# A fused two-layer Perceiver kernel: the first mixture's last eight experts in two token parts, and paired scores in the last attention

## The reference, cut to what matters

```
x = x + L0_xattn(norm(x), ctx64)     # 16 heads of 16, causal
x = x + L0_attn(norm(x))
x = x + L0_ffn(norm(x))              # mixture: 32 experts + 1 shared, top 4 of 32, silu(x W1) * (x W3) @ W2
x = x + L1_xattn(norm(x), ctx)       # 16 heads, ONE key/value head, 1601 keys per batch
x = x + L1_attn(norm(x))             # causal, 16 heads, layer norm with gamma and beta after it
x = x + L1_ffn(norm(x))              # mixture of 8 experts, gelu, top 1
```

## Time and profile before

| what | value |
|---|---|
| median of 3 runs | 552.41 us (551.35 to 553.02) |
| profiled execution, its own time | 552.53 us |
| its span, first to last instruction | 550.6 us |
| TensorE busy, share of the span | 94% |
| VectorE busy | 59% |
| ScalarE busy | 55% |
| GpSimd busy | 23% |
| mean granted TensorE clock | 0.996 |
| first mixture, steady part | 120 to 216 us of the span |
| cross attention, from its first scores | 241.35 to 400 us |
| last attention, scores to values | 415 to 442 us |

### The profile page before, as it was taken

How to read it: one execution, slowest core, us unless ns; L and a number is a source line. 1 busy time by engine, 2 the same in 40 slices (tenths; PEclk the granted TensorE clock), 3 DMA queues, 4 the chain that set the end, 5 groups by cost and what they waited for, 6 DMA issues and landing times.

```text
span 550.6 us, 15198 instructions
## 1 busy us (share of the span) xinstructions
PE 519.7 (94%) x6427; PEld 363.7 (66%) x6427; DVE 325.7 (59%) x672; ACT 300.3 (55%) x511; POOL 124.2 (23%) x217
## 2 busy tenths in 40 slices
PE   3999999889999999889999999999979999999997
PEld 2666567546665666435776767676556657999996
DVE  4455475276666665768999999998146685011011
ACT  0356566676656565358887777877714412432221
POOL 5203602644333333340000000000060043000004
PEclk9999999999999999999999999999999998999999
DMA  8914620805554453820000000000080001798823
GB/s 325 402 45 162 228 92 9 284 8 149 146 158 138 147 155 99 301 83 2 4 3 4 4 2 4 3 4 4 2 307 1 1 2 39 240 353 271 309 90 95
DMA packets 35074, 64.37 MB, mean 117 GB/s; under 512 B 3296, under 2 KB 24800, under 8 KB 34624
## 3 DMA queue, kind: packets, MB, share of 16 engines
q1 hardware_dynamic: 34480, 62.35, 34.3%
q0 software_dynamic: 384, 1.05, 0.6%
q10 hardware_dynamic: 144, 0.01, 0.0%
HBM read 59.40 MB, written 4.00 MB: 115 GB/s over the span
## 4 chain that ended last, share of the span: by engine, by line
PE 84%; DVE 8%; POOL 2%; DMA 2%; ACT 2%; issue 2%; SPq 0%; POOLq 0%; DVEq 0%; ACTq 0%
PE ps L1342 14%; PE ps L1612 10%; PE ps L1743 9%; PE ps L1711 8%; PE ps L1757 7%; PE ps L1626 7%; PE ps L1935 6%; PE ps L1443 4%; PE ps L1317 2%; PE ps L1456 2%; PE ps L1469 2%; PE ps L1423 2%; DVE region L1119 1%; DMA ctx64T<-in_ctx64T 1%; PE ps L1367 1%
## 5 line engine op out<-in xcount | busy, mean ns | idle before, releaser
L1119 DVE TENSOR_REDUCE region<-ps 128x1 f32<-128x512 f32 x192 | 124.1, 687 | 17.9 <-PE ps L1711 17.9
L807 ACT ACTIVATE region<-ps 128x1024 f32<-128x1024 f32 (+1 forms) x112 | 105.9, 963 | 19.7 <-PE ps L1743 19.2
L1711 PE MATMUL ps<-ctx_kT,region 96*32 96x512 bf16 x768 | 82.0, 383 | 2.5 <-DVE region L1119 1.8
L1743 PE MATMUL ps<-region,ctx_kT 98*32 98x512 bf16 x832 | 72.5, 381 | 0.6 <-ACT region L785 0.4
L1757 PE MATMUL ps<-region,ctx_v 128*32 128x128 f32 (+1 forms) x1664 | 70.2, 272 | 0.0
L1612 PE MATMUL ps<-region 128*128 128x512 f16 x264 | 62.9, 379 | 0.3 <-DMA region<-in_moe 0.3
L1757 PEld LDWEIGHTS ps<-region,ctx_v 128*32 128x32 f32 (+1 forms) x1664 | 56.7, 109 | 9.4 <-issue 0.3
L857 ACT ACTIVATE region<-ps,ctx_v 128x128 f32<-128x128 f32 x88 | 25.2, 369 | 60.8 <-PE ps L1342 60.8
L502 POOL TENSOR_TENSOR region<-region 128x512 f32<-128x512 f32 x33 | 38.2, 1157 | 64.7 <-ACT region L734 63.3
L1626 PE MATMUL ps<-region 128*128 128x256 bf16 x384 | 47.2, 273 | 0.9 <-DVE region L1066 0.9
L1626 PEld LDWEIGHTS ps<-region 128*128 128x128 bf16 x384 | 37.4, 98 | 12.3 <-DVE region L1066 1.5
(11 more groups left out here) (230 smaller groups left out, 839.9 us busy)
## 6 DMA issues: line engine op xcount, KB each, us to landing
region<-in_w SPq DMA_DIRECT2D x15, 1024.0 KB, 8.5
region<-in_ctxT SPq DMA_DIRECT2D x8, 1601.0 KB, 7.9
region<-gates SPq DMA_DIRECT2D x30, 256.0 KB, 3.4
ctx_kT<-in_w SPq DMA_DIRECT2D x7, 1024.0 KB, 7.3
region<-in_moe SPq DMA_DIRECT2D x33, 192.0 KB, 2.4
attn_weights<-in_wall SPq DMA_DIRECT2D x1, 2152.0 KB, 21.9
slots_x<-zeros SPq DMA_DIRECT2D x1, 1408.0 KB, 10.5
ctx_v<-in_b2row SPq DMA_DIRECT2D x1, 1024.0 KB, 4.6
```

The source lines that it names most:

```text
L807: act.activation(probs[u % NP_][:, 0:512 * n_keys], ps[:, pr:pr + n_keys, :].rearrange("p b n -> p (b n)"), ACT.Exp).then_inc(mq["exp"], 1)
L1119: ins = dve.tensor_reduce(mp[g % 2][:, j // 3, j % 3:j % 3 + 1], bank(4 + n % 2), AX.X, ALU.max)
L1711: ins = pe.matmul(ps[32 * i:32 * i + 32, at, :], QT[0:KQ, b, h + i // 2, 32 * (i % 2):32 * (i % 2) + 32], kT[0:KQ, b, 512 * c:512 * c + 51 ...
L1743: ins = pe.matmul(ps[32 * c:32 * c + 32, 2 * (u % 2) + i, :], kT[0:KQ2, b, k * P + 32 * c:k * P + 32 * c + 32], QT[0:KQ2, b, 8 * r:8 * r + ...
```

## The change

- The last `SPLIT` = 8 experts (25 to 32) are computed in two parts of 256 tokens: experts 0 to 24 whole, then 25 to 32 on tokens 0 to 255, then 25 to 32 on tokens 256 to 511. The program counts *items* i = 0 to 40 in the place of experts; `item(i)` gives the expert and the tokens. Their weights and gate rows get places of their own in `R1`, so that they stay for the second part; SP's loop over n is the same, with its wait on `m0["down"]` at n - 3.
- From item 28 on, PE runs `up(i)`, `down(i - 3)`.
- When item 32 (`A_LAST`) is done, tiles 0 and 1 are complete. DVE adds and measures tile 0 in item 35, tile 1 in item 36, scales them in items 37 and 38. PE turns tile 0 in item 39, ACT copies it there; `queries(0)` stands before `down(39)`, and the queries of tile 0 are split and turned before the last `down`.
- Tiles 2 and 3 are added and measured behind that; DVE scales them behind the first of the `maxima`.
- `chunks_by` has 15 chunks before unit 0, and 16 after it as before. Three of the six query turns (`EARLY_TURNS`) stand before unit 0, the other three in units 0 to 2. The 14 and 7 `keep_clock` matmuls around this place are gone.
- In the last attention, `pair_scores(g)` does the scores of two units at once, the units' 64-row halves in turns, and the orders of the three engines there are rearranged.

```diff
@@ sync
             for n in range(1, E0T):
+                if n == FULL:
+                    sp.wait_ge(kv["proj"], NB)
                 if n >= 4:
                     sp.wait_ge(m0["down"], n - 3)
-                    sp.dma_start(w0[n % 4], a["moe0"][n]).then_inc(w0_in[n % 4], 16)
+                    sp.dma_start(w0[place(n)], a["moe0"][n]).then_inc(w0_in[n % 4], 16)
                 if n > 2:
-                    sp.dma_start(gb[n % 4], scratch_g[n - 1:n, :].partition_broadcast(P)).then_inc(gb_in[n % 4], 16)
+                    sp.dma_start(gb[place(n)], scratch_g[n - 1:n, :].partition_broadcast(P)).then_inc(gb_in[n % 4], 16)
...
-            sp.wait_ge(m0["end"], 3)
+            sp.wait_ge(m0["end"], 2)
@@ vector, in the loop over the items, behind lo(i - 1)
+                if i == A_LAST + 3:
+                    dve.wait_ge(m0["end"], 1)
+                    dve.tensor_tensor(x[:, 0, :], sum0(0), x[:, 0, :], ALU.add).then_inc(m0["x"], 1)
+                    dve.wait_ge(m0["x"], 1)
+                    norms = [measure(x, 0, 1)]
+                if i == A_LAST + 4:
+                    dve.wait_ge(m0["down"], A_LAST + 1)
+                    dve.tensor_tensor(x[:, 1, :], sum0(1), x[:, 1, :], ALU.add).then_inc(m0["x"], 1)
+                    dve.wait_ge(m0["x"], 2)
+                    norms.append(measure(x, 1, 2))
+                if i == A_LAST + 5:
+                    scale(x, xn, mq["ln"], norms[0], 0, 1)
+                if i == A_LAST + 6:
+                    scale(x, xn, mq["ln"], norms[1], 1, 2)
@@ scalar
-            for n in range(2, E0T):
-                silu(n)
-                mid(n - 1)
-                hi(n)
-            mid(E0T - 1)
+            for i in range(2, N_I):
+                silu(i)
+                mid(i - 1)
+                hi(i)
+                if i == A_LAST + 7:
+                    act.wait_ge(mq["xt_ps"], 1)
+                    act.activation(xnT[:, :, 0:P], ps[:, 6, 0:256].rearrange("p (c q) -> p c q", c=C), ACT.Copy).then_inc(mq["xt"], 1)
@@ tensor
-            def up(n, halves_=(0, 1)):
-                wn = w0[n % 4]
+            def up(i, halves_=(0, 1)):
+                n, cc = item(i)
+                wn = w0[place(n)]
                 pe.wait_ge(w0_in[n % 4], 16 * (n // 4 + 1))
-                if n >= 2:
-                    pe.wait_ge(m0["t"], n - 1)
+                if i >= 2:
+                    pe.wait_ge(m0["t"], i - 1)
...
-            for n in range(3, E0T):
-                up(n)
-                down(n - 2)
-            down(E0T - 2)
+            for i in range(3, FULL + 2):
+                up(i)
+                down(i - 2)
+            up(FULL + 2)
+            for i in range(FULL + 3, N_I):
+                up(i)
+                down(i - 3)
...
+            down(N_I - 3)
+            queries(0)
+            down(N_I - 2)
+            pe.wait_ge(m0["x"], 2)
+            pe.wait_ge(m0["t"], N_I - 1)
+            turn_queries(0, 0, 4)
+            turn_queries(0, 1, 3)
...
-            return min(CH * NH, CH + 3 * (u + 1), 20 + -(-CH * (u + 1) // HS))
+            return min(CH * NH, CH + max(2, 3 * (u + 1)), 20 + -(-CH * (u + 1) // HS))
...
+            for n in range(2 * TT, chunks_by(-1)):
+                maxima(n, n + 1)
+                if n + 1 in EARLY_TURNS:
+                    turn_queries(*EARLY_TURNS[n + 1])
...
+            def pair_scores(g):
+                n, h, t, _ = unit(g)
+                head_done("Q", n, h)
+                head_done("K", n, h)
+                pe.wait_ge(at["z"], g)
+                for r in range(2):
+                    pe.matmul(bank(4 + r), ident_b, mask_b, start=True, stop=False, skip_group_check=True)
+                for m in range(C):
+                    for b2 in range(2):
+                        for r in range(2):
+                            q0 = (2 * t + b2) * T
+                            rr = slice(64 * r, 64 * r + 64)
+                            ins = pe.matmul(ps[64 * b2:64 * b2 + 64, 4 + r, m * 256:(m + 1) * 256],
+                                            q_T[rr, m, q0:q0 + T], k_Tm[rr, m, :, q0:q0 + T],
+                                            start=False, stop=True, skip_group_check=True)
+                ins.then_inc(at["sc"], 2)
```

More of the change, by code:

```diff
@@ L168, in build, with place, item @@
         g_s = r2(TT).rearrange("p (t e) -> p t e", e=1)
+        assert used[0] <= 11248 + 4 * H * T // 2
+        FULL = E0T - SPLIT
+        w0 += [R1[:, i * 384:(i + 1) * 384].bitcast(BF16) for i in range(SPLIT)]
+        gb += [R1[:, SPLIT * 384 + i * TOK:SPLIT * 384 + (i + 1) * TOK] for i in range(SPLIT)]
+        ITEMS = [(n, 0, TOK) for n in range(FULL)] + [(n, 256 * h, 256 * h + 256) for h in range(2) for n in range(FULL, E0T)]
+        N_I = len(ITEMS)
+        A_LAST = E0T - 1
+        def place(n):
+            return n % 4 if n < FULL else 4 + n - FULL
+        def item(i):
+            return ITEMS[i][0], slice(*ITEMS[i][1:])
         used[0] = 0
@@ L519, in _ @@
                 pool.tensor_copy(Qg[:, :, 5], Qg[:, :, 2]).then_inc(mq["qdup"], 1)
+            for i in range(N_I):
+                c = item(i)[1]
+                pool.wait_ge(m0["hi"], i + 1)
+                if i >= 2:
+                    pool.wait_ge(m0["lo"], i - 1)
+                pool.tensor_tensor(hr[i % 2][:, c], t2[i % 2][:, c], hp[i % 4][0][:, c], ALU.subtract).then_inc(m0["r"], 1)
+                if i == A_LAST + 4:
+                    root(0, 1)
+                if i == A_LAST + 5:
+                    root(1, 2)
+            queries_split(0)
+            root(2, TT)
+            for t in range(1, TT):
+                queries_split(t)
             for g in range(1, NH):
@@ L718, in _, with silu, mid, hi @@
             kv_turned(7)
[L720 to L734, removed]
+            def silu(i):
+                c = item(i)[1]
+                act.wait_ge(m0["up_a"], i + 1)
+                if i >= 2:
+                    act.wait_ge(m0["t"], i - 1)
+                act.activation(sa[i % 2][:, c], bank(2 + i % 2)[:, c], ACT.Silu, scale=1.0 / XS).then_inc(m0["silu"], 1)
+            def mid(i):
+                c = item(i)[1]
+                act.wait_ge(m0["r"], i + 1)
+                act.activation(hp[i % 4][1][:, c], hr[i % 2][:, c], ACT.Copy).then_inc(m0["mid"], 1)
+            def hi(i):
+                c = item(i)[1]
+                act.wait_ge(m0["g"], i + 1)
+                if i >= 4:
+                    act.wait_ge(m0["down"], i - 3)
+                act.activation(hp[i % 4][0][:, c], t2[i % 2][:, c], ACT.Copy).then_inc(m0["hi"], 1)
             keys_turned(6, 0)
@@ L1664, in _ @@
+            down(N_I - 3)
[5 more added lines that the diff above has]
+            turn_queries(0, 1, 3)
             for k, part in enumerate(("hi", "mid", "lo")):
-                pe.wait_ge(m0[part], E0T)
-                for t in range(TT):
-                    ins = pe.matmul(sum0(t), hp[(E0T - 1) % 4][k][:, t * P:(t + 1) * P], w0[(E0T - 1) % 4][:, 512:768],
+                pe.wait_ge(m0[part], N_I)
+                for t in (2, 3):
+                    ins = pe.matmul(sum0(t), hp[(N_I - 1) % 4][k][:, t * P:(t + 1) * P], w0[place(E0T - 1)][:, 512:768],
@@ L1776, in project_out @@
                 mm2(bank(4 + t % 2, D), lambda c: yT[:, c, t * P:(t + 1) * P], lambda c: wo(c)).then_inc(mq["out_ps"], 1)
-            queries(0)
+            maxima(0, 2)
             pe.wait_ge(mq["ln"], TT)
```

266 lines of the change are left out of this document (131 added, 135 removed).

## The result

The changed kernel takes 567.45 us (median of 4 runs, 564.72 to 568.78), the kernel before 552.71 us in the same session (4 runs, 551.35 to 556.61). The ratio, taken over all runs and not from the two medians, is 1.025, with a 95% interval from 1.018 to 1.032: slower by 10 to 17 us, where the prediction said 8.9, 561.4 us, and a range up to 566. The profiled execution took 566.29 us with a span of 564.2, 13.6 us more than the span of before, at a mean granted clock of 0.985 in place of 0.996. The other three runs had clocks of 0.978, 0.969 and 0.976.

The account below looks back on a forecast made before the run. The prediction took PE to bound the first mixture and last attention, DVE the cross attention. Its terms, 13.0 - 2.8 - 2.3 + 1.0 = +8.9 us on 552.5, gave 561.4 us, range 556 to 566.

Parts of the forecast that it names:

- Step 1: First mixture, weights of experts 26 to 32: PE waits 12.4 us in sum, 2.58 us in front of each of four.
- the late weights cost nothing: Rival for the first mixture: SP gets ahead before item 28, so the weight stalls go; 550 us, chance 0.06.
- Step 2: Second parts, items 33 to 40: ACT and DVE lead at 1.77 us an item; first maxima at S + 21.4.
- S: Start of `up(32)`, the last `up` of the first parts, put at 216.5 us with the stalls (before: 214.1).
- S + 13.8: Items 33 to 40: end of `g(40)` if PE held its pace, where the forecast itself had S + 17.5.
- the parts keep PE's pace: Rival: items 33 to 40 run at 1.52 us; 557.7 us, or 555 with the paired scores' full 4.1; chance 0.15.
- Step 3: From first maxima to first scores: tiles 2 and 3 precede the second chunk; first scores at 254.3, 13.0 us later.
- Step 4: Cross attention, units 0 to 6: fewer chunks and turns beside the units give 2.8 us back.
- Step 5: Last attention: paired scores save PE 4.1 us over four pairs; `values(22)` comes 2.3 us earlier, bounds 0 and 4.1.
- Step 6: PE's clock in the waits for late weights: if it falls, matmuls cost twice; 1.0 us, between 0 and 4.
- the clock falls in each burst: Rival: five PE bursts of 1.52 us double, 4 to 7 us in place of 1; 564.5 to 567.5, chance 0.15.

## Why the prediction was wrong

The direction and the main mechanism were right, the size wasn't, and one step, the clock, is to blame for most of it.

**Step 1, the late weights: right.** Four waits of 2.46 us against 2.58, 11.5 us in all against 12.4, and `up(32)` at 216.77 with the clock held against 216.5. The one-word change of the wait takes the loss away, with the clock that those waits cost, and the same wait alone, put into the kernel before, makes it. The rival by which the late weights cost nothing is refuted.

**Step 2, the second parts: size nearly right.** The first maxima came 21.1 us behind `up(32)`, against 21.4 (239.48 against 218.38 with the clock falling ahead of it, 237.87 against 216.77 with it held). An item took 1.64 us and not 1.77. The links `hi`, `silu`, `t`, `g`, `hi` are 0.33, 0.39, 0.46 and 0.46 us from start to start: `silu` starts 0.09 us before the record of `hi` ends, where the prediction added up full lengths. The way from `hi` over POOL and `mid` to the next `hi` (0.50, 0.70, 0.44) is as long, and the trace doesn't show which of the two binds. The prediction had not counted the second. One sum in the step is off: at PE's own pace the end would be S + 14.0, by 1.8 + 8 x 1.52, and not S + 13.8; and that rival's 555 should be 555.9, by 557.7 - (4.1 - 2.3). The rival by which the parts keep PE's pace of 1.52 us holds only while weights are the limit: with the weights in time items run at 1.53 us up to the `up` at 209.34 us, and at 1.63 and more behind it. Until then PE lived on its lead of three items, while ACT needed 1.64 for each.

**Step 3, to the first scores: right but for the clock.** It took 16.8 us with the clock held (237.87 to 254.70), predicted 16.4, and 19.4 in the changed kernel.

**Step 4: right.** 2.6 us given back, predicted 2.8. **Step 5: too high.** 1.5 us and not 2.3. Of the 4.1 us that four pairs save, PE's waits at 444.01, 445.59 and 452.52 take 1.8, one at 442.11 takes 0.2, and one of 0.9 stands ahead of the first pair; the prediction had 1.8 for all. That would leave 1.2.

**Step 6, the clock: this step failed.** It put the clock at 1.0 us and its bound at 4. Measured against the held clock it is 5.6 and 8.9 us in two sessions, each give or take 4 to 5, and 7.4 in the trace of the second; in the profiled execution of the first, the one with the best clock of four, 1.6 in front of `up(32)` (218.38 against 216.77) and 2.6 behind the first maxima (19.4 against 16.8). Two things were wrong in it. It noted that waits of 2.6 us are longer than any in its rows, and still took a value near that of rows 8, where two waits of 1.3 us cost no clock. And it looked only at step 1. Step 3 said itself that the second chunk waits for the norm of tiles 2 and 3 and never asked what PE's clock does in that wait; and the dropped `keep_clock` "cost nothing that I can find". The idle 3.28 us are there, and filled, the stretch is 1.3 us shorter even with the weights in time (18.2 against 16.9).

The rival "the clock falls in each burst", at 564.5 to 567.5, is what happened in kind and size, though not in each burst: in the profiled execution two stretches of some 7 us, the second of them behind the bursts, in other traces more. Its own working was loose: five bursts of 1.52 us that double make 7.6 us, above the 7 it allowed. The Trainium skill's page "TensorE: Matmul & The Clock Gate", section "HAM oscillation — how this bites in real kernels", describes matmul bursts of about 2 us between DMA waits of about 3 to 5 us, each burst starting at the lower clock. Its waits are longer than those of 2.46 us here, so it does not price this case, but its direction came true: the clock fell here at shorter waits too, not at each of them.

The sum with what was measured in the profiled execution: first scores +17.5 (of it 4.2 the clock), units -2.6, pairs -1.5, +13.4 against the span's +13.6. Behind the last attention two things cancel: 1.2 us less, where before had half clock at 458 us, and 1.1 us more, where PE waits for a DMA of the second mixture at 485.49 us. Predicted were 13.0 + 1.0 - 2.8 - 2.3.

**Where the intended gain went.** The parts were to fill the 27 us between the last `up` and the first scores. With the weights in time and the idle time filled they do fill it with one tile's norm and queries, but eight extra items at 1.64 us with half the columns each cost more than whole ones, and the norm of tiles 2 and 3, once beside PE's work, now stands between the first maxima and the second chunk. The first scores come no earlier: they are 54.2 and 54.7 us behind `up(24)` in two traces, against 51.8 before. The 2.6 us given back behind them are used up by that. What pays is the pairs (1.5 us) and three chunks of maxima in the idle time (1.3 us), both by the traces.

**What stays open.** Why the waits for weights cost the same kernel 1.5 us of clock in one execution and 5.3 in another, and where the 2 us come from by which the moved maxima gain more in time than in the rows.

## What to carry to other kernels

When a loop is cut into smaller items, count every prefetch wait anew in items that stand between it and its use: a wait for "four experts ago" had 3 us of work in front of its use and suddenly none. Price a wait in front of TensorE as its length plus the clock it may take from the work behind, as a range and not as one number: here 3.3 us on 9.7 us of waits in the kernel before with late loads (some 5 in its trace), and 1.5 to 5.3 us on 11.5 in the changed order. Look for such waits in every stretch that the change touches. Before dropping dummy matmuls, check what has taken their place in the new order.

## What was not expected of the hardware

- Half clock between whole experts: in the kernel before with late loads PE worked 3 us for each 2.5 us of waiting, and its clock fell three times between 208 and 233 us.
- The mean clock of one and the same kernel differs from run to run (0.969, 0.976, 0.978, 0.985 in one session), and its time by up to 4 us. The two don't go together run by run: the fastest of these four, 564.72 us, had 0.978.
- Loads issued closely behind each other land later. With the weights in time SP issued four weight loads and their gate rows in 3.2 us (186.73 to 189.97 us), and the median landing from 186 to 204 us was 3.1 us for a weight load and 4.1 for a gate row. In the changed kernel, with the same nine loads of each from 186 to 219 us, it was 2.4 and 3.4.
